# POOL begins the gathers of a unit only when all gathers of the preceding unit have landed

## The reference: what is computed

```python
q = (x @ Wq + bq).reshape(n, H, C)
k = (x @ Wk + bk).reshape(n, H, C)
v = (x @ Wv + bv).reshape(n, H, C)
attn = jnp.einsum('nhc,mhc->hnm', q, k) / np.float32(np.sqrt(C))
neg = jnp.where((adj == 0.0)[None], -jnp.inf, attn)
alpha = softmax(neg)                    # rows without an edge give 0
out = jnp.einsum('hnm,mhc->hnc', alpha, v)      # then reshaped to (n, 128)
x_r = x @ Ws + bs
beta = jax.nn.sigmoid(jnp.concatenate([out, x_r, out - x_r], axis=-1) @ Wb)
result = layernorm(x + beta * x_r + (1.0 - beta) * out)
```

## Time and profile before

| | us |
|---|---|
| median of 3 runs | 2139.12 |
| lowest, highest | 2135.24, 2142.98 |
| profiled execution, span | 2162.3 |

### The profile page before, as it was taken

How to read it: one execution, slowest core, us unless ns; L and a number is a source line. 1 busy time by engine, 2 the same in 40 slices (tenths; PEclk the granted TensorE clock), 3 DMA queues, 4 the chain that set the end, 5 groups by cost and what they waited for, 6 DMA issues and landing times.

```text
span 2162.3 us, 20047 instructions
## 1 busy us (share of the span) xinstructions
PE 1168.8 (54%) x4636; PEld 692.0 (32%) x4696; DVE 1307.7 (60%) x3389; ACT 838.7 (39%) x1595; POOL 1175.2 (54%) x1711
## 2 busy tenths in 40 slices
PE   6204656457665554558546565664755653351464
PEld 5102333224343332334324333342322332240243
DVE  6648786645875486466727564567463846582366
ACT  2305242234643263343725462455443644130112
POOL 4543655456257656666555657456445444557271
PEclk9556676667766677676857766577676766565555
DMA  8828854547676466666847765677575655224230
GB/s 316 337 61 271 285 190 179 195 165 268 224 247 222 166 238 227 230 232 249 306 150 255 266 236 198 215 253 249 202 276 184 226 200 200 68 63 103 57 91 15
DMA packets 130037, 438.70 MB, mean 203 GB/s; under 512 B 26567, under 2 KB 61198, under 8 KB 97150
## 3 DMA queue, kind: packets, MB, share of 16 engines
q1 hardware_dynamic: 76510, 297.15, 37.4%
q0 software_dynamic: 52832, 136.07, 20.8%
q10 hardware_dynamic: 576, 4.19, 0.5%
HBM read 417.93 MB, written 19.44 MB: 202 GB/s over the span
## 4 chain that ended last, share of the span: by engine, by line
DVE 27%; issue 22%; another core or an unknown queue 17%; PE 12%; ACT 10%; DVEq 9%; ACTq 1%; DMA 1%; POOL 0%; SPq 0%; POOLq 0%
ACT s_mask L1009 5%; DVE s_raw L1234 4%; DVEq L1282 3%; DVE s_kv L1232 3%; DVE s_wtop L1281 3%; PE s_acc L987 3%; DVE s_kv L1258 2%; PE s_ps_w L815 2%; DVE s_top L1325 2%; ACT s_diag L1026 2%; PE s_ps_key L893 1%; DVEq L1429 1%; DVE s_d_max L1440 1%; DVEq L1331 1%
## 5 line engine op out<-in xcount | busy, mean ns | idle before, releaser
L785 POOL DMA_INDIRECT s_kv<-kv_rows,s_rec_in x1023 | 1025.5, 1002 | 794.5 <-issue 328.8
L815 PE MATMUL s_ps_w<-s_mask,s_bit_w 128*128 128x512 bf16 x1003 | 370.9, 513 | 333.8 <-ACT s_mask L1009 172.2
L1009 ACT ACTIVATE s_mask<-s_adj_in 128x2048 bf16<-128x2048 f32 x252 | 478.3, 1900 | 138.8 <-remote 88.0
L987 PE MATMUL s_acc<-s_kv,ident 128*128 128x128 f32 x2032 | 333.0, 331 | 185.5 <-issue 112.4
L987 PEld LDWEIGHTS s_acc<-s_kv,ident 128*128 128x128 f32 x2032 | 316.4, 244 | 215.2 <-issue 123.6
L815 PEld LDWEIGHTS s_ps_w<-s_mask,s_bit_w 128*128 128x128 bf16 x1008 | 108.8, 119 | 544.5 <-issue 285.4
L1036 ACT COPY s_xs<-s_ps_x 128x128 f32<-128x128 f32 x63 | 16.5, 262 | 377.7 <-remote 181.0
L1232 DVE TENSOR_TENSOR s_kv<-s_kv,s_ps_q 128x1536 f32<-128x1536 f32 (+15 forms) x76 | 147.2, 1936 | 16.7 <-DMA s_kv<-kv_rows,s_rec_in 9.2
L1234 DVE TENSOR_REDUCE s_raw<-s_kv 128x48 f32<-128x1536 f32 (+15 forms) x76 | 147.1, 1935 | 9.8 <-issue 4.5
L1258 DVE TENSOR_TENSOR s_kv<-s_kv,s_ps_q 128x1536 f32<-128x1536 f32 (+15 forms) x76 | 146.8, 1931 | 3.5 <-ACT s_ps_q L1048 0.9
L1440 DVE TENSOR_REDUCE s_d_max<-s_ps_key 128x1 f32<-128x1024 f32 x32 | 39.2, 1225 | 158.9 <-remote 119.2
(11 more groups left out here) (281 smaller groups left out, 1573.0 us busy)
## 6 DMA issues: line engine op xcount, KB each, us to landing
s_adj_in<-in_adj SPq DMA_DIRECT2D x248, 1024.0 KB
s_kv<-kv_rows,s_rec_in POOLq DMA_INDIRECT x1023
kv_rows<-s_kv SPq DMA_DIRECT2D x16, 512.0 KB, 7.6
s_rec_in<-node_records SPq DMA_DIRECT2D x55, 106.0 KB
s_kv<-in_x_cols SPq DMA_DIRECT2D x4, 1024.0 KB, 8.8
s_adj_in<-in_adj ACTq DMA_DIRECT2D x4, 1024.0 KB
s_d_in<-in_x_cols SPq DMA_DIRECT2D x8, 512.0 KB
s_d_v<-kv_rows SPq DMA_DIRECT2D x8, 512.0 KB
```

Source lines behind the costliest of these rows:

```text
L785: nc.gpsimd.indirect_dma_start(out=kv[0:n, START[k] + s], out_offset=None, in_=kv_dram[:, :], in_offset=bass.IndirectOffsetOnAxis(ap=rec_i ...
L815: last = nc.tensor.matmul(w[:], bit_w[:, slab], mask[:, k % 2, s * WORD:(s + 1) * WORD], start=False, stop=(slab == SLABS - 1))
L987: last = nc.tensor.matmul(acc[:, c * D:(c + 1) * D], ident[:], kv[:, START[k] + s, D:2 * D], start=(s == 0), stop=(s == plain(k) - 1))
L1009: nc.scalar.activation(mask[:, q % 2], adj_in[:, q % ADJ_RING], ACT.Sign, accum_out=edges[:, t, h:h + 1]).then_inc(masked, 1)
```

## The change

In POOL's loop over the units, before the first gather of every unit but the first, POOL waits until the semaphore of the preceding unit holds the count of all its gathers. The sums of the counts are unchanged; nothing else is edited.

```diff
                     scatter_records(SCATTER_AT[k])
                 if c == 0 and p > 1:
                     pool.wait_ge(rec_loaded[p % RECS], rec_loads(p))
+                if k:
+                    pool.wait_ge(gathered[(k - 1) % FLIGHT], slots_landed(k - 1))
                 for s in range(HELD[k]):
                     if s == 0 or FREE[k][s] > FREE[k][s - 1]:
                         need(pool, summed, FREE[k][s])
```

## The result

The changed kernel takes 2071.3 us, the median of 4 runs (2052.4 to 2082.7), beside 2140.1 us for the kernel before (2135.2 to 2143.0). The ratio is 0.968, with a 95% interval of 0.961 to 0.975: faster by 68.8 us. The profiled execution is the slowest of the four, with a span of 2080.7 us, 81.6 us under the span before. Some 13 us of these 81.6 come from the choice of the two executions: the span before lies 22 us above the median of its runs, the span after 9 us above its own. This is the result under one condition.

What follows compares the result with a forecast made beforehand. The prediction took the back and forth of DVE, PE and ACT to bound the kernel, with POOL's gathers beside it. The new waits were hidden, 0 + 0 = 0 us on the path, giving 2139.1 us; the range ran from 2119 to 2163.

Steps and rivals of the forecast that it cites:

- What bounds the kernel: Whole kernel: the back and forth of DVE, PE and ACT sets the end of 2162.3 us, with POOL's gathers beside it.
- The price of a wait: POOL, at 75 unit boundaries: each new wait holds it 1.7 to 4.7 us, taken 3.3; 248 us if all exposed.
- Hidden by POOL's own waits and by the lead: POOL's 51 existing waits, 424.8 us, absorb most lateness; gathers reach DVE tens of us early, 35.5 us at unit 4.
- Rival 4: DVE comes to wait for gathers at each unit, exposing 128 to 353 us: 2267 to 2492, taken 2387; chance 0.02.
- The sum on the path, 0 + 0: The new waits at the two tight units add 0 us each to the path, so 0 us in all.
- units 17 and 23: The only tight units, scored by DVE the moment their gathers land; lateness covered by POOL's waits of 12.17 and 8.70 us.
- rival 1: POOL's lateness reaches six windows' scatters, then record loads and row turns: 20 to 28 us, 2150 to 2167, taken 2155; chance 0.27.
- rival 2: Pauses in POOL's unbroken gathers end stalls of DVE, PE and ACT, some 10 us each: 2119 to 2129, taken 2124; chance 0.17.
- The rule of the skill: Advice to issue DMAs early and wait late, speaking against the change; 75 gathers end to end an estimated 173 us.

Runs made afterwards that it cites:

- the kernel that stands for it on a full-pace chip: Changed kernel with the new wait moved to the unit before the preceding one, whose gathers have nearly always landed; 1.000 of the kernel before.
- the three first waits: Changed kernel with the new wait only ahead of units 1, 2 and 3; 0.986 of the kernel before with the slow pace, 1.0007 without.
- the idle loops: Changed kernel with 16 register additions on POOL ahead of each unit in place of the new wait; 0.980 with the slow pace, 1.005 without.
- the scatters' wait: Changed kernel where POOL also waits behind each window's scatters until they have landed; 0.956 with the slow pace, 1.088 and 1.087 without.

## Why the prediction was wrong

- **What bounds the kernel.** The forecast said DVE, PE and ACT in turn, with POOL beside them, and that held for the busy instructions. But 39% of the chain was issue and unnamed waiting, and I treated it as a property of the three engines. At unit 0 it was POOL's gathers that made such time, and POOL had 0% of the same chain: the chain follows who released whom, and the slow pace releases nobody. On chips without it the kernel before is faster by 480 us, 22%; that all of this is the slow pace is argued and not shown.
- **The price of a wait, 1.7 to 4.7 us (taken 3.3).** Fair, and in the lower half. On a full-pace chip POOL's idle time before first gathers grew by 154.5 us (73.5 to 228.0), 2.1 us for each of the 75, after what waits for records at the same places shrank. The time grew by 134 us, 1.8 us for each, which is near the 1.7 of the low end; but that is the price less what POOL's other waits still covered.
- **Hidden by POOL's own waits and by the lead.** Right on the chip of the forecast: DVE's waits for gathers rose from 9.2 to 15.7 us, under the 20 that I allowed, and POOL's waits for PE's sums shrank by 132 us. The new waits held POOL for roughly 146 us at some 50 places, in the 60 to 250 us that I expected; the named entry of 43.2 us shows a part of them. The waits for records grew by 31 us (154.7 to 185.8) where I had them shrink. But much of the lead that hid the waits was there, it seems, because the others were slow: from a unit's last gather to its score pass 55.7 us in the median in the kernel before, and 13.2 us in the kernel that stands for it on a full-pace chip. Rival 4, to which I gave 0.02, is what happens there, near the low end of its 128 to 353 us.
- **The sum on the path, 0 + 0.** This is the step that failed. I summed only what the new waits delay, at units 17 and 23, and put at nothing what a pause on POOL gives the other engines. The missing term is the stall that the pauses end: -37.7 us at unit 0 and about as much at unit 65, in a measured -68.8 us.
- **Late scatters (rival 1).** No sign of it. Of the row turns 2 in 63 wait for a record, as before:

```profile
  DMA s_rec_in<-node_records: 3.3, 2
```

- **Pauses let the others through (rival 2).** The right mechanism, at 0.17, with the wrong size and place. I priced one or two stalls of 10 us from the earlier trace rows, at units 52 and 53. I had not looked at units 0 to 2, where 56 gathers without a pause are 73 us of the timeline, and where DVE's list work was visibly slow from 88.9 us on. The busy time by stretch there, 12.7 us of DVE in the 55 us from 88 to 143, would have priced the gain at some 40 us from that place alone, an estimate from these rows and more than the 20 us that the range went below the forecast.
- **The rule of the skill.** The Trainium skill, DMA: Bandwidth & Descriptors, Rules for kernel authors, has DMAs issued early and waited for late, and by the formula in its Anatomy of one DMA (about 2.0 us fixed and the bytes over the rate) I had an estimated 173 us for 75 gathers. On the full-pace chips the trace agrees in kind, with 134 us measured. On the others the measurement goes against the rule, by 68.8 us.

## What to carry to other kernels

When much of the chain is issue time or waiting that no one is named for, look in each such stretch for what another engine does without a pause, even one with no share of the chain; here the busy time by stretch showed it and the chain didn't. Before a change is adopted for such a gain, measure it on more than one chip and at more than one time: here the same edit gave 0.968 on one and 1.081 on another, and a loop of register instructions on an idle sequencer is a cheap meter that told which of the two one had. Of the versions tried, the three first waits (0.986 and 1.0007) gain on one kind of chip and cost nothing measurable on the other, the idle loops (0.980 and 1.005) come next, and the full change (0.968 and 1.081) and the scatters' wait (0.956 and 1.088) gain more on the one and cost 8% to 9% on the other.

## What was not expected of the hardware

On chips of one kind, in long runs of indirect DMAs on POOL, the other engines get their instructions only at intervals, and so does POOL's own sequencer: register instructions of 0.03 to 0.05 us take about 0.7, and DVE ran 17 instructions in 24 us in place of 62 or 63. In the first run this began some 10 us after its start for the register loop and 22 us for DVE; it ended 2.6 us after POOL had finished the last gather. For PE and ACT the traces show idle stretches beside such runs (up to 31.5 us), and no price of one instruction. POOL's sequencer runs up to 12 gathers ahead of its engine, and holding it to 6 was no cure. On the three other chips none of this was seen, and the same kernel takes 1658 to 1661 us in place of 2140 to 2168.
